# A recommendation tower: a new order of a group's work on TensorE

## What is computed

```
e = jnp.stack([tbl_0[ids[:, 0]], ..., tbl_25[ids[:, 25]]], axis=1)     # 2048 x 26 x 128
combined = jnp.concatenate([dense_features[:, None, :], e], axis=1)   # 2048 x 27 x 128
interactions = jnp.einsum('bnd,bmd->bnm', combined, combined)
z = jnp.concatenate([dense_features, interactions[:, _TRIU_I, _TRIU_J]], axis=1)
h = jnp.concatenate([z, r_dense_features], axis=1)                    # 2048 x 607
h = jnp.maximum(h @ W_top1 + b_top1, 0.0)                             # 512
h = jnp.maximum(h @ W_top2 + b_top2, 0.0)                             # 256
y = h @ W_top3                                                        # 1
```

## Time and profile before

| what | value |
|---|---|
| median of 3 runs | 384.82 us (381.84 to 385.08) |
| the profiled execution | 385.81 us, of which the span of the profile is 383.9 us |
| mean granted TensorE clock | 0.973 of full speed |
| PE matmul busy | 333.5 us (87% of the span) |
| PE weight loads busy | 303.5 us (79%) |
| POOL busy | 269.4 us (70%) |
| DVE busy | 260.9 us (68%) |
| ACT busy | 169.3 us (44%) |

### The profile page before, as it was taken

How to read it: one execution, slowest core, us unless ns; L and a number is a source line. 1 busy time by engine, 2 the same in 40 slices (tenths; PEclk the granted TensorE clock), 3 DMA queues, 4 the chain that set the end, 5 groups by cost and what they waited for, 6 DMA issues and landing times.

```text
span 383.9 us, 13545 instructions
## 1 busy us (share of the span) xinstructions
PE 333.5 (87%) x6208; PEld 303.5 (79%) x6208; DVE 260.9 (68%) x206; ACT 169.3 (44%) x248; POOL 269.4 (70%) x277
## 2 busy tenths in 40 slices
PE   3777895949899998999899989999898989969787
PEld 2656784939898897979898879889897889859676
DVE  3999889574849865787668775777666776723322
ACT  2553563514445443545364543544354434532412
POOL 6787777777777777777777777777777777776000
PEclk9999998797999999999999999999999999997999
DMA  7996124251224322242215221341224112332020
GB/s 181 234 236 188 51 70 112 57 158 50 56 55 118 88 58 56 66 144 52 56 51 158 51 57 54 94 121 50 56 66 143 51 50 58 97 99 56 2 92 0
DMA packets 18985, 33.51 MB, mean 87 GB/s; under 512 B 5834, under 2 KB 11666, under 8 KB 18930
## 3 DMA queue, kind: packets, MB, share of 16 engines
q0 software_dynamic: 8848, 18.11, 18.2%
q1 hardware_dynamic: 10082, 14.55, 13.5%
HBM read 28.96 MB, written 3.68 MB: 85 GB/s over the span
## 4 chain that ended last, share of the span: by engine, by line
PE 40%; POOL 34%; issue 13%; DVE 7%; DMA 3%; ACT 2%; DVEq 0%; SPq 0%
POOL rows L390 34%; PE gram_ps L714 8%; PE hot_ps L684 8%; PE mlp_ps L684 8%; PE mlp_ps L720 4%; DVE one_hot L538 3%; PE transpose_ps L650 3%; PE mlp_ps L721 3%; PE mlp_ps L722 3%; DVE units L527 2%; DMA rows<-table,ids_sb 1%; PE hot_ids_ps L659 1%; PE mlp_ps L761 1%; DMA rows<-bounce 1%; DVE packed_lo L549 1%
## 5 line engine op out<-in xcount | busy, mean ns | idle before, releaser
L390 POOL DMA_INDIRECT rows<-table,ids_sb x272 | 268.5, 987 | 83.5 <-issue 80.7
L538 DVE TENSOR_TENSOR one_hot<-hot_ids_ps,row_numbers_sb 125x2048 fp32r<-125x2048 f32 x72 | 165.2, 2298 | 72.2 <-PE hot_ids_ps L659 62.7
L684 PE MATMUL hot_ps<-one_hot,table_hi 125*128 125x256 f32 x320 | 82.5, 295 | 3.4 <-issue 2.9
L684 PE MATMUL hot_ps<-one_hot,table_lo 125*128 125x256 f32 x320 | 79.6, 286 | 0.0
L684 PE MATMUL mlp_ps<-one_hot,table_hi 125*128 125x256 f32 x256 | 66.6, 297 | 11.8 <-DVE hidden_lo L569 6.4
L684 PEld LDWEIGHTS hot_ps<-one_hot,table_hi 125*128 125x128 f32 x320 | 62.1, 194 | 4.6 <-issue 4.6
L714 PE MATMUL gram_ps<-embed_t 128*27 128x27 f32 x4096 | 54.9, 195 | 11.2 <-issue 4.8
L684 PE MATMUL mlp_ps<-one_hot,table_lo 125*128 125x256 f32 x256 | 63.8, 286 | 0.0
L714 PEld LDWEIGHTS gram_ps<-embed_t 128*27 128x27 f32 x4096 | 45.0, 106 | 23.0 <-issue 15.4
L684 PEld LDWEIGHTS hot_ps<-one_hot,table_lo 125*128 125x128 f32 x320 | 62.3, 195 | 0.1
L684 PEld LDWEIGHTS mlp_ps<-one_hot,table_hi 125*128 125x128 f32 x256 | 49.9, 195 | 14.6 <-DVE one_hot L538 7.4
(11 more groups left out here) (80 smaller groups left out, 381.4 us busy)
## 6 DMA issues: line engine op xcount, KB each, us to landing
rows<-table,ids_sb POOLq DMA_INDIRECT x272
embed_t<-table SPq DMA_DIRECT2D x8, 448.0 KB
bounce<-units SPq DMA_DIRECT2D x8, 448.0 KB, 2.6
scratch<-bounce SPq DMA_DIRECT2D x7, 378.0 KB
dense_sb<-dense_t SPq DMA_DIRECT2D x8, 128.0 KB
scratch<-w SPq DMA_DIRECT2D x1, 512.0 KB, 4.8
units<-w_units SPq DMA_DIRECT2D x2, 252.0 KB
scratch<-table SPq DMA_DIRECT2D x1, 448.0 KB
```

The lines of the kernel that those rows point to most:

```text
L390: nc.gpsimd.indirect_dma_start(rows[:, t2, f - 1, :], None, tables[table], bass.IndirectOffsetOnAxis(ids_sb[:, tile, table:table + 1], 0)) ...
L538: nc.vector.tensor_tensor(one_hot[:, k % RING], ids.to_broadcast([HOT_P, HOT_STEPS, GROUP]), row_numbers_sb[:, :, None].to_broadcast([HOT_ ...
L684: last = nc.tensor.matmul(hot_bank(n), table[:, n, step, :], one_hot[:, k % RING, step, :], start=(step == 0 and table is table_hi), stop= ...
```

## The change

Only the two lists of `STEPS` are written in another order. `FIRST_STEPS`, `LAST_STEPS`, the waits, the buffers and the order on SP and POOL stay as they are.

```
 STEPS = [
-    "G0 S0 Q0 H0 M0 Q1 Q2 H1 G1 W0 Q3 H2 W1 M1 Q4 M2 W2 H3 W3".split(),
-    "G0 M3 Q0 H4 W4 M4 D0 E0 Q1 Q2 H5 W5 G1 Q3 H6 M5 Q4 H7 H8 M6".split(),
+    "G0 S0 Q0 H0 W0 H1 G1 Q1 W1 M0 M1 Q2 M2 H2 W2 Q3 H3 W3 Q4 M3 H4".split(),
+    "G0 Q0 H5 W4 M4 M5 G1 Q1 E0 Q2 H6 W5 H7 Q3 H8 Q4 D0 M6".split(),
 ]
```

## The result

| what | before | after |
|---|---|---|
| median | 384.73 us (381.84 to 385.08, 4 runs) | 412.78 us (411.31 to 413.96, 4 runs) |
| ratio to before, 95% interval | | 1.0738 (1.0678 to 1.0798) |
| profiled execution / its span | 385.81 / 383.9 us | 411.31 / 409.3 us |
| mean granted TensorE clock | 0.973 | 0.942 |
| first U / last U of groups 1 to 6 | 89.8 / 301.6 us | 89.8 / 330.8 us |

U is the end of S0 on DVE, as in the prediction. All of the loss lies between the first U and the last: up to 89.8 us the two kernels stand at the same time, then 29.2 us are lost, and 3.8 of them come back behind the last U (78.5 us to the end of the span, 82.3 before).

The account below looks back on a forecast made before the run. Gathers on POOL were taken as the floor, PE close behind. First U 88 + five chains 227 = 315, G0 of group 7 at 349.6, span 391.3, with 1.9 outside 393.2, clock + 7: 400 us, range 391 to 410.

Parts of the forecast that it names:

- first U: First end of S0 on DVE: 89.8 us in the kernel before, taken as 88 for the kernel after.
- rival "not slower": D0 or the pack early enough that S0 is never late; gathers hold PE, 384 or 386 us; decides at 42.5; chance 0.09.
- five chains: Five group periods of 45.4 us from the first U to that of group 6: 227 us, reaching 315.
- from there to G0 of group 7: From the U of group 6 to PE's G0 of group 7: 34.6 us, reaching 349.6.
- the rest: From G0 of group 7 to the span's end: 44.2 us in the old span, about 2.5 of half clock left out.
- the clock as a term of its own: PE falling to half clock behind its waits: two to three falls of 2.7 us in groups 1 to 6, + 7.
- (a): DVE after U: two one-hots, two copies and a low half, then M2 starts on PE; 6.3 us.
- (b) to (d): M2 to M3, PE running through to Q3, then ids, one-hots and D0 on DVE; D0 ends 36.4 us after U.
- (e): D0's end to next U: load issue, pack to `bounce` and `scratch`, landing, S0 on ACT and DVE; 8.7 us.
- closed chain of 45.4 us a group: One period from U to U through DVE, PE, SP and the pack; 2.9 us more than the gathers allow.
- forecast of 409 by that page: Second rival: by the skill page all six groups fall to half clock, 393.2 + 16 = 409; four or more falls, chance 0.17.
- chain of 46.4 with four falls: Bound from above on the group period; 398 us for the kernel, 409 with four clock falls.

Follow-up runs that it names:

- filled kernel: Kernel after, with thrown-away products put into PE's waits in groups 1 to 6; 409.9 us, 1.0629 of before.

## Why the prediction was right and where it failed

**What bounds the kernel: right.** With D0's effect taken away, by D0's place or by SP's order, the time is 383 to 385 us and the gathers set it. With it, POOL waits for PE and no longer leads. One reading was too strong: POOL did wait in the kernel before, six times for PE, but never longer than its own 0.3 us.

**The direction and the mechanism: right.** The pack behind the load, the load behind D0 (0.37 us from load to pack, forecast 0.4), S0 waiting on ACT and DVE, PE standing at M0 and M2. Two experiments, each with one edit, took back all of it. The rival "not slower" fails where the text put its condition: the chain is over 42.5, by 5.7 us.

**The size: too small by 11.3 us against the profiled execution (411.3 to 400), 12.8 against the median.** In the terms of the sum: first U + 1.8 (89.8, not 88); five chains + 14 (5 x 48.2 = 241, not 227); from there to G0 of group 7 + 1.2 (366.6 - 330.8 = 35.8, not 34.6); the rest + 1.0 (42.7, not 41.7); the clock as a term of its own - 7, since its falls are inside the rows just named. That is 11.0. Another 0.1 lies outside the span, and the sum of 400.2 was rounded to 400.

The chain, step by step, in the mean of the five intervals between the U of groups 1 and 6:

| step | forecast | measured |
|---|---|---|
| (a) U to M2 | 6.3 | 7.3 (6.5, 7.9, 6.6, 8.8, 6.5) |
| (b) to (d) M2 to the end of D0 | 30.1 to 30.5 | 31.2 |
| (e) D0 to U | 8.7, with 0.1 for hand-overs | 9.7 |
| sum | 45.4 | 48.2 |

So the step of the prediction that failed is its closed chain of 45.4 us a group, which took 48.2: 1.0 us too little in (a), 0.9 in (b) to (d) and 0.9 in (e), paid five times.

**Step (a) failed in the even groups.** It counts two one-hots back to back. There the second has to wait for a product of ids that PE issues behind G1, and that product waits for the first one-hot that S0 has held up. So PE stands ahead of M0, at a place that I had passed over, and a hand-over there and back lies in DVE's chain. I had followed the products of ids at the end of a group and not at its head. At full clock this is 1.0 us (7.3 in the filled kernel). The rest up to 8.8 is the half clock: in group 4 the low half of M0 is there at 240.5, and PE, still slow in M1 and Q2, starts M2 only at 241.9. In odd groups (a) holds within 0.3.

**Steps (b) to (d) nearly held, but their small errors add up to 0.9 us.** M2 to M3 took 6.6 to 6.9 (forecast 6.6) but for one with a fall, 8.4; M3 to G0 3.5 (3.4) and G0 to G1 7.2 (7.1); G1 to the end of D0 13.2 to 13.9, where 13.0 to 13.4 was forecast. One fall spread over five intervals is 0.3 of the 0.9; the rest is some 0.1 for each joint.

**Step (e) was mis-sized by 0.9 us,** by taking two DMA times from a kernel in which they ran at another moment. `units` to `bounce` took 3.1 to 3.6 behind the load, against the 2.62 of the earlier trace rows; with the load behind the pack, at the same place, it took 2.75, so there the load is shown as most of the difference. It is not the whole story, since 3.7 also came with no load ahead. The landing took 3.2 to 4.8 beside gathers, mean 4.0, against the 3.43 of the earlier trace rows that come from the end, where no gathers run. ACT's S0 to U took 1.82 instead of 2.13 and gave 0.3 back.

**The clock: more falls than forecast, each much cheaper.** I set aside 2.7 us for each of two or three falls. The rows above show five in six groups. Both rows of the prediction showed a fall behind a stretch with waits, which spoke for more than the two or three that I took. But the falls cost 3.7 us of the chain in all by the estimate above, and keeping the clock up gave back 2.9. The price of 2.7 would hold if PE were what is waited for in that stretch. Here a third of these stretches is PE's own wait (in group 2, 4.04 of 6.80 us are busy), and then DVE's one-hots are the chain up to M2 in the odd groups. The Trainium skill (TensorE: Matmul & The Clock Gate, "HAM oscillation") has the penalty as half of the time at half clock: for the 37 us at half clock in the rows above that makes 19 us, an estimate by that page. On how often it falls the trace agrees with that page; on the price it does not, in a kernel where another engine sets the pace of the stretch. That the forecast of 409 by that page came near the result is no merit of its price: the five chains were 14 us longer, and some 10 of them for other reasons.

**The range.** Its upper end was 410, just over the 409 of a chain of 46.4 with four falls. The uncertainty on the chain was taken as 0.05 for each of 20 joints in both directions. What it lacked was room for a wait that I had not seen and for DMAs in another setting, and these are not noise: both lengthened the chain in the mean, and neither is as likely to shorten it.

**What would show it:** the DMA to `bounce` 0.37 us behind the load: as said. PE's waits: at M0 only in groups 3 and 5 (3.9 and 2.4 us, about 2 forecast), at M2 in groups 1, 3 and 5 (3.3, 1.2 and 1.8, where 3.4 was forecast), in the even groups at the ids instead. G0 to G0 45 to 46 us: no, 47.2 to 49.0. POOL waiting for `transposed` little and late, PE hardly for gathers: as said. More stretches at half clock: as said, but beginning at M0 or ahead of it, not at M2.

## What to carry to other kernels

Before a consumer is moved to a later place, look for who waits for it on a queue that serves others too: here a prefetch that nobody needed until D0 two groups later stood in order ahead of a pack that was needed at once, and swapping the two on SP turned 412.8 us into 383.0. When a chain closes on itself, walk each of its engines through one whole period for every kind of period (even and odd groups here), with every wait that its instructions have, and read transfers from a moment with the same neighbours; a missed wait is paid in every turn. A fall of the clock is to be priced by who is waited for in that stretch, and filling a wait with idle work pays only where PE is the chain and the filling ends in time.

## What the runs showed of the hardware

**Gathers are lengthened by subtractions on DVE.** A gather takes 0.94 us on POOL, but longer when it starts while `packed_lo` runs, which reads two tensors in SBUF. Kernel after, a gather on POOL and then DVE:

```profile
281.63 1.42 POOL L390 DMA_INDIRECT rows<-table,ids_sb  x1 [0.30 <-issue]
```

```profile
281.27 0.96 DVE L549 TENSOR_TENSOR packed_lo<-scratch,packed_hi 126x768 fp32r<-126x768 f32 x1 [7.03 <-ACT packed_hi L449]
```

The gather ends at 283.05, 0.82 us after DVE's instruction. In the trace of before the gather that starts at 258.24 takes 1.74 us in the same way, and ends 0.82 us after a `packed_lo` that ends at 259.16. In the two kernels 13 gathers start while a `packed_lo` of 768 columns runs; 12 of them end 0.81 or 0.82 us after it, and the one that starts 0.01 us behind it takes 0.94. A gather that is already under way is not lengthened: this one starts 0.46 us ahead of the `packed_lo` at 135.05.

```profile
134.59 0.94 POOL L390 DMA_INDIRECT rows<-table,ids_sb  x1 [0.30 <-issue]
```

It is as if a gather's work could begin only when DVE was through. The Trainium skill (GPSIMD Engine Reference, 1. Specifications) says that GpSimd and VectorE share their SBUF interfaces and collide when a DVE instruction has two SBUF inputs; the trace agrees. That this is the mechanism was not tested.

**A fall of the clock can be moved, and land worse.** With 30 thrown-away products the stretch at half clock went from 357.5, where it cost 0.4 us (G0 to the last pack 7.0 us with it, 6.6 without), to 374.0, where it cost 1.5.
